# An exchange of score halves in pieces of 128 KB instead of 64 KB, issued ahead of the loads of x

## What is computed

```
h = max(layernorm(x), 0)
q = h @ Wq.T + bq;  k = h @ Wk.T + bk;  v = h @ Wv.T + bv
a = q @ k.T * (1/16) + adj + adj
out = x + softmax(a, axis=-1) @ v
```

## Time and profile before

| | us |
|---|---|
| median of 3 runs (lowest, highest) | 717.09 (715.97, 719.55) |
| profiled execution, its own time | 716.58 |
| its span, first to last instruction | 714.8 |
| PE busy | 691.9 (97%) |
| DVE busy | 595.0 (83%) |
| ACT busy | 435.5 (61%) |
| POOL busy | 429.2 (60%) |

### The profile page before, as it was taken

The page is one execution under the profiler, slowest core; times in us unless marked ns, Lnnn a source line. Parts: engine busy times, 40 slices in busy tenths (PEclk is TensorE's granted clock), DMA queues, the critical chain, the costliest instruction groups (busy, mean ns, idle before and its releaser), DMA issues.

```text
span 714.8 us, 14696 instructions
## 1 busy us (share of the span) xinstructions
PE 691.9 (97%) x4799; PEld 474.8 (66%) x4799; DVE 595.0 (83%) x1284; ACT 435.5 (61%) x732; POOL 429.2 (60%) x434
## 2 busy tenths in 40 slices
PE   5789998999999999999999999999999999999997
PEld 4556555666666667667667667666667666766786
DVE  4899686778898888788788888898888888887895
ACT  4898664665656565656666575656566665656530
POOL 1879415365755667664657565566647475655686
PEclk9999999999999999999999999999999999999999
DMA  8558799988978888897988898888879888878473
GB/s 283 174 140 265 198 235 264 265 216 227 241 212 257 232 242 214 238 242 221 270 221 241 244 246 221 247 213 247 232 218 270 217 238 245 242 220 225 122 171 95
DMA packets 93244, 161.06 MB, mean 225 GB/s; under 512 B 20976, under 2 KB 41840, under 8 KB 93168
## 3 DMA queue, kind: packets, MB, share of 16 engines
q1 hardware_dynamic: 68432, 126.41, 63.3%
q10 hardware_dynamic: 24736, 33.72, 17.7%
HBM read 80.35 MB, written 8.39 MB: 124 GB/s over the span
## 4 chain that ended last, share of the span: by engine, by line
PE 81%; DVE 5%; DMA 4%; SPq 3%; ACTq 2%; issue 2%; ACT 2%; POOL 0%; DVEq 0%; POOLq 0%
PE bank L1461 43%; PE bank L1528 37%; ACTq L803 2%; SPq L436 2%; DVE stats L1060 1%; DVE rows L1142 1%; DMA rows<-in_adj 1%; PE bank L1475 1%; DMA rows<-in_x 1%; SPq L425 1%; DMA g_scratch<-xT 1%; DMA v_sb<-rows 1%; SPq L407 1%; DMA xT<-rows 1%; DMA rows<-rows 1%
## 5 line engine op out<-in xcount | busy, mean ns | idle before, releaser
L641 POOL TENSOR_TENSOR wT<-xT,wT 128x512 f16<-128x512 f32 x233 | 269.4, 1164 | 233.5 <-ACT wT L821 229.5
L1461 PE MATMUL bank<-v_sb,wT 128*128 128x256 f16 x2796 | 343.9, 273 | 0.0
L1528 PE MATMUL bank<-top,a_op 128*128 128x512 f16 x1344 | 331.6, 379 | 4.8 <-DVE rows L1093 3.0
L1461 PEld LDWEIGHTS bank<-v_sb,wT 128*128 128x128 f16 x2796 | 274.2, 98 | 81.2 <-issue 0.3
L821 ACT CAST wT<-xT 128x512 f16<-128x512 f32 x233 | 139.6, 611 | 127.0 <-PE bank L1461 74.6
L1528 PEld LDWEIGHTS bank<-top,a_op 128*128 128x128 f16 x1344 | 131.1, 98 | 113.8 <-DVE rows L1093 3.3
L792 ACT ACTIVATE rows<-rows,exp_bias,exp_scale 128x1024 f32<-128x1024 f32 x128 | 158.7, 1240 | 63.6 <-issue 33.7
L1115 DVE CUSTOM_DVE_ANT_0 rows<-bank,rows 128x512 f32<-128x512 f32 x256 | 173.7, 680 | 12.1 <-PE bank L1528 3.4
L1142 DVE STREAM_TRANSPOSE rows<-rows 128x1024 f32<-128x1024 f32 x128 | 158.4, 1239 | 3.4 <-ACT rows L792 3.4
L1100 DVE SCALAR_TENSOR_TENSOR rows<-rows,adj_scale,bank 128x512 f32<-128x512 f32 x64 | 47.7, 746 | 48.9 <-PE bank L1528 48.8
L783 ACT ACTIVATE rows<-rows,adj_scale 128x512 f32<-128x512 f32 x64 | 46.1, 722 | 34.5 <-POOL wT L641 20.3
(11 more groups left out here) (115 smaller groups left out, 451.7 us busy)
## 6 DMA issues: line engine op xcount, KB each, us to landing
rows<-in_adj SPq DMA_DIRECT2D x128, 512.0 KB, 5.4
xT<-rows SPq DMA_DIRECT2D x488, 64.0 KB, 3.1
xT<-rows ACTq DMA_DIRECT2D x488, 64.0 KB, 3.4
rows<-in_x SPq DMA_DIRECT2D x8, 512.0 KB, 5.5
xy<-in_x SPq DMA_DIRECT2D x32, 128.0 KB, 4.5
g_scratch<-xT SPq DMA_DIRECT2D x16, 256.0 KB, 4.4
g_pair<-g_scratch SPq DMA_DIRECT2D x15, 256.0 KB, 3.6
out_y<-xy SPq DMA_DIRECT2D x30, 128.0 KB, 5.5
```

Source lines behind the costliest of these rows:

```text
L641: nc.gpsimd.tensor_tensor(split_piece(m, 1), exchanged(m), split_piece(m, 0), ALU.subtract).then_inc(split_lo, 1)
L1461: return nc.tensor.matmul(out_ap, stationary, moving, start=first, stop=last)
L1528: last = nc.tensor.matmul(ps[:], s, mv, start=first and k == 0, stop=k == 2, skip_group_check=True)
```

## The change

A source row of a part is 4 KB, 2 KB for each of its two chunks. The changed kernel sends both with one DMA: 32 source partitions, 4 KB of each, to 64 partitions, 128 KB. Key 32 j + s of chunk k lands on partition 2 s + k of its half; `move_v` writes v to every second partition to match. A unit takes 4 + 4 DMAs instead of 8 + 8, the semaphores count 64 instead of 128 a unit, and `exchange_b` has four calls of one DMA where it had four of two. In SP's period `exchange_a` moves ahead of `load_xy` and `load_g`.

```diff
             def move_v(g):
                 first = g // HALF_CHUNKS * BLOCKS
-                group = slice(g % HALF_CHUNKS * Q, (g % HALF_CHUNKS + 1) * Q)
+                k = g % HALF_CHUNKS
+                group = slice(k // 2 * 2 * Q + k % 2, (k // 2 + 1) * 2 * Q, 2)
...
             def exchange_a(u):
                 sp.wait_ge(turned, 2 * u + 1)
                 arrival_free(sp, u)
                 row = unit_row(u, 0)
-                for k in range(2):
-                    for i in range(P // Q):
-                        sp.dma_start(arrivals(u)[k * Q:(k + 1) * Q, i].rearrange("p j q -> p (j q)"),
-                                     row[i * Q:(i + 1) * Q, k * CH:(k + 1) * CH]).then_inc(landing(u, 0), 16)
+                for i in range(P // Q):
+                    sp.dma_start(arrivals(u)[0:2 * Q, i].rearrange("p j q -> p (j q)"),
+                                 row[i * Q:(i + 1) * Q, :]).then_inc(landing(u, 0), 16)
...
             def refill(u, part):
-                    sp.wait_ge((moved_b if part else moved_a)[u % XT], 128 * (u // XT + 1))
+                    sp.wait_ge((moved_b if part else moved_a)[u % XT], 64 * (u // XT + 1))
...
             def period(n):
+                if unit_in_range(u):
+                    exchange_a(u)
                 if n % QUADS in (0, 1) and 2 <= p < PAIRS:
                     load_xy(2 * p + n % QUADS)
                 if n % QUADS == 0 and p + 1 < PAIRS:
                     load_g(p + 1)
-                if unit_in_range(u):
-                    exchange_a(u)
...
-            def exchange_b(u, k, first):
+            def exchange_b(u, i):
                 if unit_in_range(u):
                     act.wait_ge(turned, 2 * u + 2)
                     arrival_free(act, u)
-                    row = unit_row(u, 1)
-                    for i in range(first, first + 2):
-                        act.dma_start(arrivals(u)[(2 + k) * Q:(3 + k) * Q, i].rearrange("p j q -> p (j q)"),
-                                      row[i * Q:(i + 1) * Q, k * CH:(k + 1) * CH]
-                                      ).then_inc(landing(u, 1), 16)
+                    act.dma_start(arrivals(u)[2 * Q:P, i].rearrange("p j q -> p (j q)"),
+                                  unit_row(u, 1)[i * Q:(i + 1) * Q, :]).then_inc(landing(u, 1), 16)
```

More of the change, by code:

```diff
@@ L363, in arrival_free @@
                 for v in (PERIODS - 8, PERIODS - 7):
-                    eng.wait_ge(moved_b[v % XT], 128 * (v // XT + 1))
+                    eng.wait_ge(moved_b[v % XT], 64 * (v // XT + 1))
             if k > 0:
                 for v in (PERIODS - 6, PERIODS - 5):
-                    eng.wait_ge((moved_b if k == 2 else moved_a)[v % XT], 128 * (v // XT + 1))
+                    eng.wait_ge((moved_b if k == 2 else moved_a)[v % XT], 64 * (v // XT + 1))
         def landing(u, part):
@@ L951, in _ @@
             high_query(2)
-            exchange_b(0, 0, 0)
+            exchange_b(0, 0)
             evict_g(4, 1)
             evict_g(5, 0)
-            exchange_b(0, 0, 2)
+            exchange_b(0, 1)
             high_v(13)
@@ L961, in _ @@
             evict_g(5, 1)
-            exchange_b(0, 1, 0)
+            exchange_b(0, 2)
             exponential(2, 0)
@@ L965, in _ @@
             evict_g(6, 0)
-            exchange_b(0, 1, 2)
+            exchange_b(0, 3)
             exponential(2, 1)
@@ L973, in _ @@
             high(1)
-            exchange_b(1, 0, 0)
+            exchange_b(1, 0)
             scale_adj(6)
-            exchange_b(1, 0, 2)
-            exchange_b(1, 1, 0)
-            exchange_b(1, 1, 2)
+            exchange_b(1, 1)
+            exchange_b(1, 2)
+            exchange_b(1, 3)
             def period(n):
@@ L1014, in _ @@
             u = PERIODS - EXP_LAG
-            exchange_b(u - 1, 0, 0)
+            exchange_b(u - 1, 0)
             high(LATE - 3)
-            exchange_b(u - 1, 0, 2)
+            exchange_b(u - 1, 1)
             high(LATE - 2)
@@ L1020, in _ @@
             exponential(u, 0)
-            exchange_b(u - 1, 1, 0)
+            exchange_b(u - 1, 2)
             exponential(u, 1)
-            exchange_b(u - 1, 1, 2)
+            exchange_b(u - 1, 3)
             exponential(u + 1, 0)
-            exchange_b(u, 0, 0)
+            exchange_b(u, 0)
             exponential(u + 1, 1)
-            exchange_b(u, 0, 2)
+            exchange_b(u, 1)
             exponential(u + 2, 0)
-            exchange_b(u, 1, 0)
+            exchange_b(u, 2)
             exponential(u + 2, 1)
-            exchange_b(u, 1, 2)
+            exchange_b(u, 3)
             exponential(u + 3, 0)
-            exchange_b(u + 1, 0, 0)
+            exchange_b(u + 1, 0)
             exponential(u + 3, 1)
-            exchange_b(u + 1, 0, 2)
-            exchange_b(u + 1, 1, 0)
-            exchange_b(u + 1, 1, 2)
+            exchange_b(u + 1, 1)
+            exchange_b(u + 1, 2)
+            exchange_b(u + 1, 3)
             for v in (u + 2, u + 3):
-                for k in range(2):
-                    exchange_b(v, k, 0)
-                    exchange_b(v, k, 2)
+                for i in range(P // Q):
+                    exchange_b(v, i)
             store_rest(TILES - 2)
```

24 lines of the change are left out of this document (12 added, 12 removed).

## The result

| us | before | changed |
|---|---|---|
| median of 20 runs each, same chip | 717.24 | 714.02 |
| lowest, highest | 714.10, 719.84 | 710.34, 720.79 |
| profiled execution, its span | 716.58, 714.8 | 712.38, 710.6 |

The ratio is 0.9964, 95% interval 0.9948 to 0.9980. The time is inside the range of the prediction, but 3.2 us over its figure, and just short of the 0.5% from which it spoke of faster. The two profiled executions lie 4.2 us apart, the medians 3.2. All ratios leave out executions over 1.5% above the fastest of their kernel, which only e2 has: four of twelve, its profiled one among them.

A forecast was written before the change was run, and what follows sets the result against it. PE was taken to bound the kernel, idle only at 122 us and the end. Gains of 4.5 + 1.8 = 6.3 us off the profiled 716.58 gave 710.3, as a median 710.8 us; range 708.8 to 716.0.

The forecast's parts named there:

- What bounds the kernel: PE, busy 97% of the span and all of the loop; gains lie only where PE idles.
- the stop: PE's wait at 122 us for DVE and a load of adj for period 8; 2.99 us, 4.5 with clock loss.
- The price of a piece: Issuing a 128 KB piece keeps a queue 0.66 us (0.54 to 0.84); landing takes 3.7 us.
- So the load is issued at about 113.8 instead of 119.18 and lands at 119.1 instead of 124.5: Load of adj for period 8 on SP's queue, before PE's wait at 122 us; eight issues replace sixteen.
- the term of 4.5 us: Gain at PE's 122 us wait, counted as wholly gone with its clock loss; 3.7 at the other end.
- rival 1: Exchange goes by bytes, not pieces: large pieces hold a queue twice as long, both waits stay; median 717.1, chance 0.12.
- The end: Last exchange pieces on ACT land at 699.5 instead of 705.15, POOL starts sooner; 1.8 us gained (1.6 to 2.0).
- The loop: nothing, gain or loss: SP and ACT each save about 2.6 us of queue a period, but PE is never idle there: 0 us.
- a new wait of PE in the loop, on `rows<-in_adj`: Sign that the forecast is wrong: PE waiting in the loop for loads of adj; no size given.
- SP's new order: nothing: In SP's period the exchange goes ahead of the loads of x and g; no gain or loss.
- Nearly 4 us to spare: In SP's period, the later load of g still lands nearly 4 us before POOL's first use at 338.12.
- rival 2: Only one of the gains at the 122 us wait and the program's end, or part; median 713.5, chance 0.14.

The follow-up runs named there:

- e2: Changed kernel with SP's old order (loads of x and g ahead of the exchange), large pieces kept: 1.0023 of the kernel before, 717.98 us.
- e1: Kernel before with SP's new order alone (exchange ahead of the loads of x and g), 64 KB pieces: 1.0005, 717.26 us.
- e3: Changed kernel with each piece cut in two (16 source rows of 4 KB, 64 KB), new order and partitions kept: 1.0011, 717.52 us.
- e14: Changed kernel with two start-list loads of adj cut to 128 of 1024 columns, 0.9 MB less moved, output wrong: 715.35 us, one run.
- e12: The changed kernel measured again, unaltered: 0.9971 of the kernel before, 714.25 us.
- e4: e3 with 128 KB pieces for the first and last four units only: 0.9954 of the kernel before, 712.9 us.
- e6: e4 with loop pieces of 32 rows x 2 KB onto every second partition: 0.9972 of the kernel before, 713.91 us.
- e5: Changed kernel with SP's loads of x and g moved behind the two refills of each period: 1.0315 of the kernel before, 739.48 us.
- e16: e3 with 128 KB pieces everywhere on ACT, and on SP only at the two ends: 0.9976 of the kernel before, 714.96 us.
- e7: e6 without large pieces at the end, so 128 KB pieces in the first four units alone: 0.9983 of the kernel before, 714.89 us.
- e15: e3 with 128 KB pieces everywhere on SP, and on ACT only at the two ends: 0.9980 of the kernel before, 714.93 us.
- e9: e4 with unit 1's exchange one place earlier in SP's start list, ahead of a 512 KB refill: 0.9968 of the kernel before, 713.65 us.
- e10: e9 with the load for period 8 also ahead of unit 2's exchange in SP's start list: 0.9984 of the kernel before, 714.44 us.
- e13: e4 with the load of period 8's other tile moved behind the load of period 8 in SP's start list: 0.9959, 713.06 us.
- e11: Changed kernel with unit 1's exchange one place earlier in SP's start list: 0.9981 of the kernel before, 714.10 us.
- e8: The kernel before run once more, unaltered, for a second trace: 714.1 us, one run.

## Why the prediction was wrong in size

**What bounds the kernel**: right. Nothing was gained in the loop; both gains are where PE idled.

The step that failed is the time of the load at the stop, and with it the largest term; a second term was put at nothing and was a loss.

**The price of a piece**: 0.66 us was taken, 0.62 measured in the loop (4 in 2.49), so an issue does not cost by its bytes there. At the start it was 1.0 us (8 in 8.03), beyond the upper end of 0.84, and the eight saved 3.6 us of queue instead of 6.4.

**"So the load is issued at about 113.8 instead of 119.18 and lands at 119.1 instead of 124.5"**: this step failed, and with it the term of 4.5 us. The load left at 118.26 and landed at 122.78. The 3.7 us of landing was a median over the span, put on pieces issued into a stretch where the DMA engines are busy at 1.02; the last piece of unit 1, issued at 111.59, took 6.65. Here rival 1 was right in its effect, though not in its reason: the exchange went by its bytes. Counted from its first issue, the part of unit 1 that SP sends had landed after 9.1 to 10.2 us in the four executions with small pieces at the start (both before, e1, e3) and after 9.4 to 10.6 us in the nine with large ones and the same list; with 0.9 MB less on the way (e14) after 6.9. So the load was issued 1.1 us earlier on average (118.75 for 119.82) and landed 1.0 us earlier, where 5.4 was forecast. The rule of the Trainium skill, page "DMA: Bandwidth & Descriptors", section "Issuing engines are not separate DMA queues", that the time to initiate a DMA is usually small relative to the DMA itself, agrees with the trace in this stretch: 11.67 us of issues became 8.03, and the landing of unit 1 moved from 116.98 to 118.24, the wrong way. It does not hold at the end, where twenty issues of 0.73 us in a row were the path.

**The worth of the stop** was read from one execution. Before, the stop cost 5.18 us in one and 2.56 in the other, 2.97 in e1 and 5.22 in e3: mean 4.0 with small pieces at the start. With large ones and the same list it cost 0.96, 1.63, 1.52, 1.31, 1.03, 2.02, 1.92, 4.59 and 6.01 (changed, e12, e4, e6, e2, e5, e16, e7, e15): mean 2.3. The term is 1.7 us, not 4.5. In the ledger's terms, 5.2 us were to be gained, all of the stop: 1.2 of them were not there on average before, and 2.3 stayed. These are thirteen executions, and each group has a low cluster (0.96 to 2.97) and a high one (4.59 to 6.01), so 1.7 is an estimate, with a standard error of 0.9; with the column before 85 us added, which moves against this one, it is 1.5. The pair of the result had 4.2 us, near the forecast, but by luck: a costly execution before against the cheapest with this list after, and 1.0 us of the shorter wait was PE's later arrival.

**The end: 1.8 us.** Right. Small pieces there lose 1.95 to 3.95 us (five executions, mean 2.75), large ones 0.07 to 1.35 (all the others, thirteen, e9 to e14 with 0.45 to 0.90 among them; mean 0.64): 2.1 us.

**"The loop: nothing, gain or loss."** Wrong: the changed kernel loses 1.82 and 1.29 us there, against 0.25 to 0.34 in the seven executions with small pieces in the loop and the old start list. That PE was never idle there bounded the gain, but not the loss. That the large pieces are the cause is likely and not shown: e10 and e13 have small pieces in the loop and lose 2.58 and 1.76 us, by the same wait (for e10 the view has "PE bank L1537 <- DVE rows L1102: 1.7, 2, 1.0"), at 144 us among other places, and e11 has large ones and loses 0.44. (The 1.06 of e9 is the rest of its stop.) The timeline of the changed kernel at its one stop of over 1 us:

```profile
514.81 0.91 SPq L401 DMA_DIRECT2D out_y<-xy  x2
...
524.68 0.34 SPq L395 DMA_DIRECT2D xy<-in_x  x1
525.44 0.34 SPq L416 DMA_DIRECT2D g_pair<-g_scratch  x1
525.83 1.26 SPq L388 DMA_DIRECT2D rows<-in_adj  x2
...
531.75 0.94 SPq L388 DMA_DIRECT2D rows<-in_adj  x2
...
534.81 0.75 DVE L1089 SCALAR_TENSOR_TENSOR rows<-rows,adj_scale,bank 128x512 f32<-128x512 f32 x1 [2.91 <-DMA rows<-in_adj]
...
535.62 1.47 PE L1524 MATMUL bank<-top,a_op 128*128 128x512 f16 x6 [1.11 <-DVE rows L1089]
```

The store issued at 514.81 takes nearly 10 us, the load of x waits for it, the refills leave behind it, and a load of 8 us is then late for DVE. The prediction named this as what would make it wrong, "a new wait of PE in the loop, on `rows<-in_adj`", and said that no row gave a reason: rows 5 did not, since medians of the kernel before say nothing of how its slow landings grow.

**SP's new order: nothing.** Right for small pieces (e1), wrong as a statement on the change: with large pieces it is worth some 4 us (e2). The waits for x and g which the prediction thought covered came, without reaching PE:

```profile
ACT h_tile L823 <- DMA xy<-in_x: 41.9, 17, 5.5
...
POOL comb L608 <- DMA g_pair<-g_scratch: 23.2, 10, 5.5
```

The kernel before has neither in its loop. "Nearly 4 us to spare" for g became a wait of up to 5.5; e1, with the new order and small pieces, has none for g and 0.9 us for x, so the order alone does not bring it.

**The sum.** 1.7 + 2.1 - 1.3 = 2.5 us by the ledger, against 3.2 measured between medians; without the loop's loss 3.8, against e4's 0.0046 x 717 = 3.3. Forecast was 6.3. In its outcome this is rival 2, one gain and part of the other (713.5), which had a chance of 0.14; its stated reason, that landings stretch where the engines are full, fits most of the traces but not e14, where the load took 6.2 us at a share of 0.88.

## What to carry to other kernels

Read a stop from more than one execution before it becomes a term of a sum: here a second execution of the same kernel had half of it. A median landing time is no forecast for one DMA in a stretch with more bytes on the way: here fewer or earlier issues brought it forward by about 1 us where 5 were forecast. A longer time from issue to landing is not yet a later landing: look whether the issue came forward. Where an engine is covered in the loop, it is enough to change the transfer where it is on the path (e4: the first and last four units).

## What the runs showed of the hardware

- *Rows of 4 KB that go to two partitions are cut to the same packets.* The trace has 34,944 packets of 2 KB in every kernel, large pieces or small. But one takes 140 ns on average in the changed kernel and in e3, 137 in e4, against 122 before and in e6, whose loop pieces read 2 KB a row. So it is the source rows of 4 KB, not the size of the DMA, that lengthen the packets on average (the median packet of e3, 119 ns, is that of the kernel before, 118); the DMA share rises from 0.85 to 0.91 in e3. Why was not tested.
- *Large pieces on SP lengthen the time from issue to landing of the loads behind them, and little else.* Adj takes 8.1 us, or 7.9 (e15), against 6.1 when only ACT's pieces are large (e16) and 6.3 with none (e3), at the same bytes. The load is issued that much sooner behind the same exchange, and from its first piece on the medians are alike (12.3, 12.5, 12.7 and 12.6 us). The share is 0.96 and 0.99 against 0.87 and 0.91.
- *Small packets go with the number of DMAs.* The page counts 85,048 packets where it counted 93,244, and those under 512 B fell by 8,192 (20,976 to 12,784): 16 for each of the 512 DMAs less. What the exchange moves is the same.
- *The clock.* At the stop PE's granted clock fell behind waits of 2.44 us (e3), 2.62 (e7), 2.82 (e11), 2.99 (before), 3.60 (e9) and 3.64 (e15), and not behind 2.33 (e1) or shorter ones: there six matmuls take 1.47 us, in e11 2.74, at the lower of the two levels, 1.2 GHz, for most of them. What PE lost around the stop beyond the wait itself was 1.8 us in five of the six and 2.7 in e9, against 0.2 in e1 and e8. So a few tenths of a us in a landing can be worth more than their size. But the length of the wait does not decide alone: in the loop the clock fell behind a wait of 2.26 us (e5, at 517.53, six matmuls in 2.65 us) and stayed full behind one of 2.88 (e2, at 509.82, six in 1.47).
